# Reciprocals of dt taken row by row instead of in two halves, in a Mamba-2 and mixture-of-experts block

## The chip, the cores and the metric

The kernel runs on one core of a Trainium2 chip, as one launch. The metric is the device time of one execution in microseconds (us). The engines are named as in the profile: PE is TensorE (PEld its weight loads), DVE is VectorE, ACT is ScalarE, POOL is GpSimd, and SP is the queue that issues most DMAs. All data of the computation are 32-bit floats, apart from some counters and masks.

## What is computed

Four rows of 512 tokens with 256 channels pass through an adaLN block: a modulated layer norm, a Mamba-2 mixer, a gated residual, and then a second modulated layer norm with a top-2 mixture of 8 experts and its residual. The part that the change touches is the mixer's `x / dt`:

```python
dt = softplus(A_log)                       # (4, 512, 64): one value per token and head
x_in = x / dt[..., None]                   # x: (4, 512, 64 heads, 8)
y_ssm = ssd_chunk_scan(x_in * dt[..., None], -dt, Bm, Cm, CHUNK)
Du = D[None, None, :, None] * x_in
yf = (y_ssm + Du).reshape(b, L, D_INNER)
out = einsum('bld,ed->ble', yf * silu(z + z_bias), out_proj_w)
```

The scan itself needs only `x`; `1/dt` is wanted for the term `D * x / dt` that is added to the scan's result. `D` has 64 values, one for each head.

## The kernel before, in words

**Tiles.** The 2048 tokens are 16 tiles of 128, four to a row, tile `n = 4*b + i` for row `b` and place `i`. Tokens lie on the partitions, so `dt`, `fu`, `fv` and `fq` are tensors of 128 x 16 tiles x 64 heads (L324 for `fq`). `fq` holds `D / dt`.

**Order of the work.** All five engines run through one list of steps, made by `program_order` (L96 to L148), and each engine takes from a step what is its own, in that order. Engines wait for each other through counting semaphores alone. The list begins with the first norm, row 0's projections and the factors made of `dt`. Then, for each row, four rounds follow, one for each token tile. A round has the steps `tr` (transposes to token layout and the products C times B), `bt`, `z` (y of the tile before, transposed and gated), `state`, `out` (its output projection and residual), `norm` (its second layer norm) and `y` (the tile's scan result), with gaps between them. The gaps are filled by the next row's projections (`p`), its own z projections, and steps of the experts, as the table `GAPS` says. Row 3 has the experts' matmuls in its gaps.

**Taps.** A projection tile (`proj`, L1703 on PE) goes through ACT (L1143, newest tap with bias), then DVE adds the three older taps of the convolution in three instructions (L1315), and ACT applies silu (L1072). DVE does not do the taps in the step `proj` itself but at the end of the next step of the list, or at the next `proj` (L1307, `pending`).

**The reciprocals.** `1/dt` is the step `d_dt`. DVE takes the reciprocal (L1383) and signals `inverse_ready`; POOL multiplies by `D` (L984) and signals `q_ready`. There are two such steps, each for 8 tiles (2 rows, 512 elements a partition): one in the first list, ahead of row 0's last z projection and tile 0, and one after the step `y` of tile 2 of row 0.

```python
if (slot, i, kind) == (0, 2, "y"):
    steps.append(("d_dt", 1))
```

**What uses them.** In the step `tr` POOL waits for `q_ready`, then writes `xv = xtok * fv` (L1013) for the scan and `xtok = xtok * fq` in place (L1017). The wait is before both:

```python
pool.wait_ge(q_ready, n // 8 + 1)
pool.wait_ge(xtok_ready, n + 1)
```

PE needs `xv` for the state products (L1802) and for the scan's products within a chunk (L1833). DVE scales the scan's result by `fu` (L1432) and adds `xtok` (L1439, the "sum of y" below, `ysum_ready`); PE transposes that in the next round's `z` (L1850), DVE gates it (L1448), PE multiplies with the output weights (L1859), and DVE adds the residual (L1457).

**The second norm of a tile.** In the step `out` DVE takes BN_STATS and BN_AGGR of the new residual (L1264, L1265). In the step `norm` POOL makes `rst` from the variance with two instructions (L947, L948), and DVE normalizes with it to `xn` (L1292), at the head of the same step. In the step `y` POOL makes the scaled rows for the experts from `xn` (L957, L958). At the start of a row, in the step `fold_out`, POOL also multiplies the output weights `wog` by a gate (L1025).

**Names of the other steps and tensors.** `gm` are the masked products of C and B (DVE L1394); `st` is the state at the chunk bounds (DVE L1415, L1419, L1420, which reads `scr` and `dec`); `btok` (ACT L1206) is B in token layout; `xtok` (ACT L1199) is x in token layout.

Of the kernel before, what the change touches and what calls it, by code (L numbers as in the profile page):

```python
# [24 lines left out]
P = 128  # L25
BATCH, SEQ, DM = 4, 512, 256
# [69 lines left out]
def program_order():  # L96
# [13 lines left out]
    for slot in range(BATCH):  # L110
# [5 lines left out]
        for i in range(TPB):  # L116
            prev = (slot, i - 1) if i else (slot - 1, TPB - 1)
            gap = 0
            for kind in ("tr", "", "bt", "z", "", "state", "", "out", "", "norm", "y", ""):
                if not kind:  # L120
                    steps += filling(slot, GAPS[slot][i][gap], nxt, z_own, pair_work)
                    gap += 1
                elif kind in ("z", "out", "norm"):
                    if prev[0] >= 0:
                        steps.append((kind,) + prev)
                else:
                    steps.append((kind, slot, i))
                if (slot, i, kind) == (0, 2, "y"):
                    steps.append(("d_dt", 1))
                if i == 0 and kind == "y":  # L130
                    steps.append(("fold_out", slot))
# [130 lines left out]
def adaln_block(nc, x_d, cT_d, wmod_d, win_d, small_d, wo_d, wg1_d, wg2_d,  # L262
# [16 lines left out]
    with ExitStack() as ctx:  # L279
# [116 lines left out]
        fv_f = fv[:, :, :].rearrange("p i h -> p (i h)")  # L396
        fq_f = fq[:, :, :].rearrange("p i h -> p (i h)")
        ident = cst[:, C_ID:C_ID + P]
# [538 lines left out]
        def _(pool):  # L937
# [32 lines left out]
            for step in STEPS:  # L970
# [8 lines left out]
                elif kind == "d_dt":  # L979
                    h = step[1]  # L980
                    fq_h = fq[:, 8 * h:8 * h + 8, :]
                    pool.wait_ge(ld["small"], 16)
                    pool.wait_ge(inverse_ready, h + 1)
                    pool.tensor_tensor(fq_h, fq_h, dh.rearrange("p (o h) -> p o h", o=1).to_broadcast([P, 8, N_HEAD]),  # L984
                                       ALU.mult).then_inc(q_ready, 1)
# [15 lines left out]
                elif kind == "tr":  # L1001
# [3 lines left out]
                    pool.wait_ge(uv_ready, 4)  # L1005
                    pool.wait_ge(q_ready, n // 8 + 1)
                    pool.wait_ge(xtok_ready, n + 1)
# [245 lines left out]
        def _(dve):  # L1253
# [69 lines left out]
            for step in STEPS:  # L1323
# [56 lines left out]
                elif kind == "d_dt":  # L1380
                    h = step[1]
                    dve.wait_ge(dt_ready, h + 1)
                    dve.reciprocal(fq_f[:, halves(h)], dt_f[:, halves(h)]).then_inc(inverse_ready, 1)  # L1383
                elif kind == "proj" and step[2] < N_CONV:
# [650 lines left out]
```

## Time and profile before

| | us |
|---|---|
| median of 3 runs | 457.52 |
| the three runs | 454.83, 457.52, 464.47 |
| the profiled execution, its own time | 455.36 |
| its span, from first to last instruction | 453.1 |
| mean granted TensorE clock, share of full | 0.936 |

The span is what the trace shows; about 2.3 us of the time lie around it. From the trace's stretches: the first norm and row 0's projections take up to 82 us, the token tiles of row 0 from there to 143, those of row 1 to 213, of row 2 to 286, row 3 with the experts of rows 0 to 2 to 414, and row 3's own experts the rest. Times of trace rows count from the span's start.

### The profile page before, as it was taken

To read this page: it belongs to the slowest core of one execution; us is meant where nothing else is said; L and a number is where in the kernel's file an instruction comes from. 1 tells how busy PE (TensorE), PEld (TensorE's weight loads), DVE (VectorE), ACT (ScalarE), POOL (GpSimd) and SP (SyncE) were. 2 spreads that over 40 slices of the span, in tenths; PEclk is the share of its full clock that TensorE was granted. 3 is DMA by queue.
4 is the path that set the end of the run, shared out by engine and by line. 5 is a ranking of instruction groups with operands and counts; after the bars stand their busy time and mean duration, and the time that the engine had idled before them with its cause. 6 is when DMAs were issued, how large, how long until landed. Compare 5 with 4: busy or idle time off the path is not lost.

```text
span 453.1 us, 8779 instructions
## 1 busy us (share of the span) xinstructions
PE 389.9 (86%) x3224; PEld 250.1 (55%) x3224; DVE 285.2 (63%) x624; ACT 166.7 (37%) x291; POOL 138.8 (31%) x170
## 2 busy tenths in 40 slices
PE   7799698888878999698998969696979886978997
PEld 4378343455635556356655545463867775664365
DVE  4733648898895558998458987733645531152566
ACT  1516757542423253333343323122432534443310
POOL 1300200423134334042771131653245100715230
PEclk9859799999989999999999899977999998888999
DMA  8999911100000102000321000036367579877123
GB/s 255 368 385 387 377 65 23 60 14 2 3 2 2 52 21 61 1 2 3 109 57 61 0 4 1 25 119 199 86 207 255 173 224 352 282 265 243 47 70 116
DMA packets 45820, 56.41 MB, mean 124 GB/s; under 512 B 4228, under 2 KB 37676, under 8 KB 45764
## 3 DMA queue, kind: packets, MB, share of 16 engines
q1 hardware_dynamic: 38276, 44.38, 30.0%
q0 software_dynamic: 2304, 6.29, 4.3%
q10 hardware_dynamic: 5184, 4.98, 3.2%
q8 instruction: 36, 0.59, 0.6%
q14 instruction: 20, 0.16, 0.1%
HBM read 32.82 MB, written 22.82 MB: 123 GB/s over the span
## 4 chain that ended last, share of the span: by engine, by line
PE 53%; DVE 27%; issue 7%; DMA 4%; ACT 4%; SPq 3%; POOL 1%; DVEq 0%; ACTq 0%; POOLq 0%
PE ps L1703 14%; DVE conv L1315 13%; PE ps L1759 4%; PE ps L1859 4%; PE ps L1904 4%; PE ps L1922 3%; PE ps L1768 3%; PE ps L1782 3%; PE ps L1629 2%; PE ps L1833 2%; PE ps L1663 2%; DMA conv<-pair_rows 2%; PE ps L1750 2%; PE ps L1802 2%; DMA conv<-x 1%
## 5 line engine op out<-in xcount | busy, mean ns | idle before, releaser
L1703 PE MATMUL ps<-hT,win 128*128 128x512 f32 x256 | 134.3, 653 | 9.1 <-DVE conv L1315 7.9
L1315 DVE SCALAR_TENSOR_TENSOR conv<-ps,small,conv 128x511 f32<-128x511 f32 x144 | 106.8, 746 | 33.8 <-ACT conv L1143 30.4
L1703 PEld LDWEIGHTS ps<-hT,win 128*128 128x128 f32 x256 | 47.8, 204 | 54.0 <-issue 38.0
L1143 ACT ACTIVATE conv<-ps,small 128x512 f32<-128x512 f32 x48 | 37.2, 775 | 78.7 <-PE ps L1703 78.7
L947 POOL TENSOR_SCALAR rst<-mv 128x1 f32<-128x1 f32 x16 | 3.6, 225 | 126.5 <-DVE mv L1265 126.5
L1072 ACT ACTIVATE conv<-conv 128x512 f32<-128x512 f32 x48 | 29.7, 624 | 33.1 <-DVE conv L1315 33.0
L1058 POOL DMA_INDIRECT conv<-pair_out,ysloti x24 | 24.1, 1006 | 42.3 <-DVE x L1586 28.3
L1859 PE MATMUL ps<-wog,yT 128*128 128x256 f32 x128 | 31.2, 387 | 1.6 <-issue 1.6
L1859 PEld LDWEIGHTS ps<-wog,yT 128*128 128x128 f32 x128 | 24.2, 195 | 10.8 <-issue 8.2
L1629 PE MATMUL ps<-cst,conv 128*128 128x128 f32 x128 | 20.6, 285 | 10.4 <-ACT conv L1072 4.5
L1629 PEld LDWEIGHTS ps<-cst,conv 128*128 128x128 f32 x128 | 15.1, 145 | 23.6 <-issue 13.8
L1039 POOL DMA_INDIRECT pair_rows<-hs,sloti x24 | 24.3, 1012 | 6.9 <-issue 6.9
L1759 PE MATMUL ps<-conv,hs 128*128 128x128 f32 x152 | 22.8, 301 | 4.1 <-DMA hs<-w_pair 2.8
L1013 POOL TENSOR_TENSOR xv<-xtok,fv 128x512 f32<-128x512 f32 x16 | 17.5, 1096 | 26.9 <-ACT xtok L1199 26.8
L1759 PEld LDWEIGHTS ps<-conv,hs 128*128 128x128 f32 x152 | 20.4, 210 | 6.3 <-issue 4.8
L1802 PEld LDWEIGHTS ps<-xv,btok 64*64 64x64 f32 x448 | 12.9, 140 | 18.6 <-issue 11.2
L1148 ACT ACTIVATE sz<-ps,small 128x512 f32<-128x512 f32 x16 | 10.9, 684 | 32.3 <-PE ps L1703 20.3
L1802 PE MATMUL ps<-xv,btok 64*64 64x64 f32 x448 | 15.1, 231 | 8.0 <-ACT btok L1206 3.3
L1768 PE MATMUL ps<-hs,conv 128*128 128x256 f32 x76 | 19.8, 397 | 0.9 <-DVE hT L1572 0.8
L1833 PE MATMUL ps<-xv,gm 64*64 64x64 f32 x512 | 18.4, 221 | 2.2 <-PE ps L1820 1.0
L1173 ACT ACTIVATE conv<-ps,bupt 128x128 f32<-128x128 f32 x38 | 11.9, 363 | 20.8 <-PE ps L1759 20.8
L1833 PEld LDWEIGHTS ps<-xv,gm 64*64 64x64 f32 x512 | 16.2, 134 | 4.4 <-PE ps L1820 4.4
(189 smaller groups left out, 615.4 us busy)
## 6 DMA issues: line engine op xcount, KB each, us to landing
pair_rows<-zrow SPq DMA_DIRECT2D x1, 12288.0 KB, 43.3
hs<-w_pair SPq DMA_DIRECT2D x38, 256.0 KB, 4.3
conv<-pair_rows SPq DMA_DIRECT2D x38, 128.0 KB, 2.6
pair_out<-conv ACTq DMA_DIRECT2D x18, 256.0 KB, 4.7
conv<-x SPq DMA_DIRECT2D x4, 512.0 KB, 7.7
wog<-w_out_T SPq DMA_DIRECT2D x4, 512.0 KB
win<-w_in_T SPq DMA_DIRECT2D x2, 512.0 KB, 7.8
hs<-w_mod SPq DMA_DIRECT2D x1, 1024.0 KB, 9.6
```

The costliest lines, as they stand in the source:

```text
L1039: pool.indirect_dma_start(xs_d, bass.IndirectOffsetOnAxis(routed(sloti, b, k, i), 0), hb[b][:, i, :], None, bounds_check=N_SLOT - 1, oob_i ...
L1058: pool.indirect_dma_start(yg[:, n % 4, k, :], None, ys_d[g], bass.IndirectOffsetOnAxis(routed(ysloti, b, k, i), 0), bounds_check=GROUP_TIL ...
L1072: act.activation(dst, dst, ACT.Silu).then_inc(silu_done, 1)
L1143: act.activation(conv[:, b % 2, m, :], bank(step), ACT.Identity, bias=cb[:, m:m + 1], scale=cw[:, m, KSIZE - 1:KSIZE]).then_inc(tap0, 1)
L1315: dve.scalar_tensor_tensor(out=dst, in0=bank(("proj", b, m))[:, 0:SEQ - s], scalar=cw[:, m, KSIZE - 1 - s:KSIZE - s], in1=dst, op0=ALU.mul ...
L1629: ins = pe.transpose(bank(job)[:, tile_cols(j)], conv[:, b % 2, base + j, tile_cols(i)], ident)
L1703: ins = pe.matmul(bank(step), win[:, k, m * P:(m + 1) * P], hT[:, k, b * SEQ:(b + 1) * SEQ], start=(k == 0), stop=(k == KD - 1))
L1759: ins = pe.matmul(bank(step)[:, tile_cols(t % 2)], wt[:, t % W_RING, k * P:(k + 1) * P], hg[:, q % 2, k, tile_cols(t % QUAD)], start=(k == ...
L1768: ins = pe.matmul(bank(step)[:, j * DM:(j + 1) * DM], hq[:, q % 2, tile_cols(t % QUAD)], wt[:, t % W_RING, KD * D_EXP:], start=True, stop= ...
L1802: ins = pe.matmul(ps[64 * par:64 * par + 64, bank_of[job], j * CHUNK:(j + 1) * CHUNK], btok[rows, n % 2, g * 64:(g + 1) * 64], xv[rows, n ...
L1833: last = pe.matmul(ps[rows, bank_of[job], j * CHUNK:(j + 1) * CHUNK], gm[rows, n % 2, par, j * CHUNK:(j + 1) * CHUNK], xv[rows, n % 2, g * ...
L1859: ins = pe.matmul(bank(step)[:, 0:DM], yT[:, n % 2, m, :], wog[:, m, :], start=(m == 0), stop=(m == CT_ - 1))
```

## The change

The step `d_dt` is for one row now, with 4 tiles and 256 elements a partition. Row 0's stands where the first half stood. The others stand in tile 2 of the row ahead (rows 1, 2 and 3 in tile 2 of rows 0, 1 and 2), directly before the step `norm`. POOL's wait in `tr` is for its own row's product.

```diff
@@ program_order, in the loop over rows and tiles
                 elif kind in ("z", "out", "norm"):
+                    if kind == "norm" and i == 2 and slot + 1 < BATCH:
+                        steps.append(("d_dt", slot + 1))
                     if prev[0] >= 0:
                         steps.append((kind,) + prev)
                 else:
                     steps.append((kind, slot, i))
-                if (slot, i, kind) == (0, 2, "y"):
-                    steps.append(("d_dt", 1))
@@ POOL
                 elif kind == "d_dt":
-                    h = step[1]
-                    fq_h = fq[:, 8 * h:8 * h + 8, :]
+                    b = step[1]
+                    fq_b = fq[:, b * TPB:(b + 1) * TPB, :]
                     pool.wait_ge(ld["small"], 16)
-                    pool.wait_ge(inverse_ready, h + 1)
-                    pool.tensor_tensor(fq_h, fq_h, dh.rearrange("p (o h) -> p o h", o=1).to_broadcast([P, 8, N_HEAD]),
+                    pool.wait_ge(inverse_ready, b + 1)
+                    pool.tensor_tensor(fq_b, fq_b, dh.rearrange("p (o h) -> p o h", o=1).to_broadcast([P, TPB, N_HEAD]),
                                        ALU.mult).then_inc(q_ready, 1)
@@ POOL, step "tr"
-                    pool.wait_ge(q_ready, n // 8 + 1)
+                    pool.wait_ge(q_ready, b + 1)
@@ DVE
                 elif kind == "d_dt":
-                    h = step[1]
-                    dve.wait_ge(dt_ready, h + 1)
-                    dve.reciprocal(fq_f[:, halves(h)], dt_f[:, halves(h)]).then_inc(inverse_ready, 1)
+                    b = step[1]
+                    dve.wait_ge(dt_ready, b // 2 + 1)
+                    dve.reciprocal(fq[:, b * TPB:(b + 1) * TPB, :], dt[:, b * TPB:(b + 1) * TPB, :]).then_inc(inverse_ready, 1)
```

A line number of the changed kernel is one less than that of the kernel before from the removed line on. Since `d_dt` is a step of its own, the taps that were pending at `norm` in tile 2 of row 0 are now done at the end of `d_dt`. On DVE, from BN_AGGR of tile 2 of row 0 on, there stood (conv is written by the three taps):

```order
L1265 BN_AGGR mv<-bns 128x2 [waits dve_chain]
L1292 TENSOR_SCALAR xn<-x,mv,rst 128x256 [waits xn_used,var_ready,rstd_ready]
L1315 SCALAR_TENSOR_TENSOR conv<-ps,small,conv 128x511 [waits tap0_written]
L1315 SCALAR_TENSOR_TENSOR conv<-ps,small,conv 128x510 [waits taps_added]
L1315 SCALAR_TENSOR_TENSOR conv<-ps,small,conv 128x509 [waits taps_added]
```

and behind the sum of y of that tile, the reciprocal of 512 elements:

```order
L1439 TENSOR_TENSOR ytok<-ytok,xtok 128x512 [waits ytok_ready,xq_ready]
L1383 RECIPROCAL fq<-dt 128x512 [waits dt_ready]
L1394 TENSOR_TENSOR gm<-ps,cst 128x256 [waits bank3_full,bank6_full]
L1394 TENSOR_TENSOR gm<-ps,cst 128x256 [waits bank4_full]
L1315 SCALAR_TENSOR_TENSOR conv<-ps,small,conv 128x511 [waits tap0_written]
```

Now there stands, from BN_AGGR on:

```order
L1264 BN_AGGR mv<-bns 128x2 [waits dve_chain]
L1382 RECIPROCAL fq<-dt 128x256 [waits dt_ready]
L1314 SCALAR_TENSOR_TENSOR conv<-ps,small,conv 128x511 [waits tap0_written]
L1314 SCALAR_TENSOR_TENSOR conv<-ps,small,conv 128x510 [waits taps_added]
L1314 SCALAR_TENSOR_TENSOR conv<-ps,small,conv 128x509 [waits taps_added]
L1291 TENSOR_SCALAR xn<-x,mv,rst 128x256 [waits xn_used,var_ready,rstd_ready]
L1431 TENSOR_TENSOR ytok<-ps,fu 128x4x64 [waits bank5_full]
```

The reciprocal stands ahead of the taps, the taps ahead of `xn`, and none stands between the sum of y and `gm`. In tile 2 of row 1 (and of row 2, where it reads the same but for a name), DVE had

```order
L1315 SCALAR_TENSOR_TENSOR conv<-ps,small,conv 128x511 [waits tap0_written]
L1315 SCALAR_TENSOR_TENSOR conv<-ps,small,conv 128x510 [waits taps_added]
L1315 SCALAR_TENSOR_TENSOR conv<-ps,small,conv 128x509 [waits taps_added]
L1292 TENSOR_SCALAR xn<-x,mv,rst 128x256 [waits hb_ready,xn_used,var_ready,rstd_ready]
L1432 TENSOR_TENSOR ytok<-ps,fu 128x4x64 [waits bank5_full]
```

and now has

```order
L1314 SCALAR_TENSOR_TENSOR conv<-ps,small,conv 128x511 [waits tap0_written]
L1314 SCALAR_TENSOR_TENSOR conv<-ps,small,conv 128x510 [waits taps_added]
L1314 SCALAR_TENSOR_TENSOR conv<-ps,small,conv 128x509 [waits taps_added]
L1382 RECIPROCAL fq<-dt 128x256 [waits dt_ready]
L1291 TENSOR_SCALAR xn<-x,mv,rst 128x256 [waits hb_ready,xn_used,var_ready,rstd_ready]
L1431 TENSOR_TENSOR ytok<-ps,fu 128x4x64 [waits bank5_full]
```

so here the taps already stood ahead of `xn`, and the reciprocal is between them. On POOL, in the same place of row 1, there stood from the tile before's `xtok` on

```order
L1017 TENSOR_TENSOR xtok<-xtok,fq 128x512 [waits xv_ready]
L947 TENSOR_SCALAR rst<-mv 128x1 [waits var_ready]
L948 TENSOR_TENSOR rst<-rst,half 128x1 [waits pool_chain]
L957 TENSOR_TENSOR hs<-xn,hm 128x256 [waits ld_hm,xn_ready]
L958 TENSOR_TENSOR hs<-hs,hm 128x256 [waits pool_chain]
```

and now

```order
L1016 TENSOR_TENSOR xtok<-xtok,fq 128x512 [waits xv_ready]
L983 TENSOR_TENSOR fq<-fq,small 128x256 [waits inverse_ready,ld_small]
L946 TENSOR_SCALAR rst<-mv 128x1 [waits var_ready]
L947 TENSOR_TENSOR rst<-rst,half 128x1 [waits pool_chain]
L956 TENSOR_TENSOR hs<-xn,hm 128x256 [waits ld_hm,xn_ready]
L957 TENSOR_TENSOR hs<-hs,hm 128x256 [waits pool_chain]
```

POOL's product with `D`, which waits for the reciprocal, is now ahead of `rst`, in rows 0, 1 and 2 alike. PE, ACT and SP have the same instructions in the same order as before.

## Rows read from the trace of the kernel before

**Rows 1.** The page, part 1: busy us, share of the span and instructions.
```profile
PE 389.9 (86%) x3224; PEld 250.1 (55%) x3224; DVE 285.2 (63%) x624; ACT 166.7 (37%) x291; POOL 138.8 (31%) x170
```
**Rows 2.** Chain that ended last: start us, us, engine, tile, line.
```profile
126.64 3.36 DVE fq L1383
...
131.35 1.09 POOL xv L1013
```
**Rows 3.** DVE's timeline, row 0: start us, us, line, operation, count, [idle before, releaser].
```profile
82.20 3.34 DVE L1383 RECIPROCAL fq<-dt 128x512 f32<-128x512 f32 x1
...
87.33 2.31 DVE L1315 SCALAR_TENSOR_TENSOR conv<-ps,small,conv 128x511 f32<-128x511 f32 x3 [1.18 <-ACT conv L1143]
...
90.57 1.35 DVE L1420 TENSOR_TENSOR st<-scr,dec 128x256 f32<-128x256 f32 x1
```
**Rows 4.** PE's timeline at the start of tile 3 of row 0.
```profile
127.33 1.88 PE L1703 MATMUL ps<-hT,win 128*128 128x512 f32 x4
132.53 0.68 PE L1802 MATMUL ps<-xv,btok 64*64 64x64 f32 x16 [3.32 <-POOL xv L1013]
133.14 3.54 PE L1703 MATMUL ps<-hT,win 128*128 128x512 f32 x4
```
**Rows 5.** DVE's timeline, tiles 2 and 3 of row 0.
```profile
121.43 0.18 DVE L1265 BATCH_NORM_AGGREGATE mv<-bns 128x2 f32<-128x6 f32 x1
122.62 0.41 DVE L1292 TENSOR_SCALAR xn<-x,mv,rst 128x256 f32<-128x256 f32 x1 [1.01 <-POOL rst L948]
...
129.90 0.69 DVE L1394 TENSOR_TENSOR gm<-ps,cst 128x256 f32<-128x256 f32 x2
...
138.59 0.42 DVE L1457 TENSOR_TENSOR x<-ps,x 128x256 f32<-128x256 f32 x1 [2.16 <-PE ps L1859]
```
**Rows 6.** POOL's timeline, row 0.
```profile
89.28 2.36 POOL L1025 TENSOR_TENSOR wog<-wog,gates 128x1024 f32<-128x1024 f32 x1
...
123.11 0.73 POOL L957 TENSOR_TENSOR hs<-xn,hm 128x256 f32<-128x256 f32 x1 [0.53 <-DVE xn L1292]
...
130.13 1.27 POOL L984 TENSOR_TENSOR fq<-fq,small 128x512 f32<-128x512 f32 x1 [5.47 <-DVE fq L1383]
```
**Rows 7.** Timelines of POOL, DVE and PE, tiles 2 and 3 of row 1.
```profile
195.71 0.57 POOL L948 TENSOR_TENSOR rst<-rst,half 128x1 f32<-128x1 f32 x1
...
200.99 1.07 POOL L1013 TENSOR_TENSOR xv<-xtok,fv 128x512 f32<-128x512 f32 x1
...
198.58 0.41 DVE L1292 TENSOR_SCALAR xn<-x,mv,rst 128x256 f32<-128x256 f32 x1
...
199.75 0.69 DVE L1439 TENSOR_TENSOR ytok<-ytok,xtok 128x512 f32<-128x512 f32 x1
...
208.47 0.42 DVE L1457 TENSOR_TENSOR x<-ps,x 128x256 f32<-128x256 f32 x1 [0.52 <-PE ps L1859]
...
200.01 0.60 PE L1629 MATMUL ps<-cst,conv 128*128 128x128 f32 x4
200.59 0.63 PE L1850 MATMUL ps<-cst,ytok 128*128 128x128 f32 x4
```
**Rows 8.** Timelines of DVE and PE, tile 3 of row 2 and tile 0 of row 3.
```profile
269.66 0.69 DVE L1439 TENSOR_TENSOR ytok<-ytok,xtok 128x512 f32<-128x512 f32 x1
...
268.26 0.63 PE L1629 MATMUL ps<-cst,conv 128*128 128x128 f32 x4 [1.59 <-issue]
...
269.72 3.59 PE L1703 MATMUL ps<-hT,win 128*128 128x512 f32 x4
...
273.68 0.60 PE L1850 MATMUL ps<-cst,ytok 128*128 128x128 f32 x4
...
295.01 1.61 PE L1802 MATMUL ps<-xv,btok 64*64 64x64 f32 x32 [3.32 <-ACT btok L1206]
296.55 3.78 PE L1703 MATMUL ps<-hT,win 128*128 128x512 f32 x4
```
**Rows 9.** One stretch: busy us of PE, PEld, DVE, ACT, POOL; PEclk, DMA share, GB/s.
```profile
133.00:137.00 4.00, 4.00 (x13) 1.84 (x10) 3.32 (x6) 0.76 (x2) 0.58 (x1) 0.57 0.02 6
```

More of the change, by code:

```diff
@@ L396, in adaln_block @@
         fv_f = fv[:, :, :].rearrange("p i h -> p (i h)")
-        fq_f = fq[:, :, :].rearrange("p i h -> p (i h)")
         ident = cst[:, C_ID:C_ID + P]
```

## The prediction

> **What bounds the kernel now.** I read the page first, then the chain of waits, then the timelines of single engines around the two reciprocals and around the places to which the diff moves them. TensorE (PE) is busy for 86% of the span and VectorE (DVE) for 63% [rows 1]; neither share says what a change in one stage is worth. In the loop over token tiles the chain passes back and forth between the two: DVE's three older taps of a projection tile, PE's projections, and again the taps. So an operation counts only where its engine is the late one. The second reciprocal is such a place. It stands in the chain for 3.36 us, and behind it POOL's products for the next tile, `xv` with 1.09 us the last of them [rows 2]; then PE goes on. The first reciprocal is in no such place, as the next part shows.
>
> **Part 1, the first reciprocal (before tile 0 of row 0).** It runs from 82.20 for 3.34 us. DVE then has two short `gm` products and idles 1.18 us until ScalarE has written a conv tile, at 87.33 [rows 3]. Half as many elements make the reciprocal 1.67 us instead of 3.34 (in proportion; a fixed part could make it a little more). DVE saves 1.67 us and waits longer by as much, for the wait was there already. Worth here: 0. But POOL gets its input 1.67 us earlier and its own product is shorter: 1.27 us for 512 elements a partition [rows 6], and about 0.73 us for 256, the length of a product of that size on POOL at 123.11 [rows 6]; bounds 0.64 (half) and 1.27. So POOL is some 2.2 us ahead, and its scaling of `wog`, now from 89.28 to 91.64 [rows 6], ends near 89.4. In that time DVE's product `st<-scr,dec`, from 90.57, takes 1.35 us [rows 3], where a sum of 256 elements takes 0.42 [rows 5]. If `wog` is done before, DVE gets 0.93 us back, on a stretch in which DVE never idles until PE waits for it. I take -0.9, with 0 as the other end.
>
> The Trainium skill, SBUF — State Buffer, section "Who interferes with whom", says that a VectorE instruction with two SBUF inputs and a GpSimd instruction that reads SBUF exclude each other for the whole of the one that started first. The trace agrees so far: the slow product has both inputs in SBUF and ends when `wog` has ended. By that rule the 0.9 is gained as soon as `wog` ends first; without it the sum would be 0.9 higher.
>
> **Part 2, the second reciprocal leaves the end of tile 2 of row 0.** The order now has a reciprocal of half the size between BN_AGGR and the taps. Before, DVE idles 1.01 us ahead of `xn` for POOL's `rst` [rows 5]. After, the reciprocal starts where the idle time started, at 121.61; the taps follow; and `xn` comes behind them. POOL's product and `rst` need 0.14 + 0.73 + 0.9 = 1.8 us after the reciprocal (0.14 is the step from its end to POOL's start at 130.13, 0.9 is the rest of the 1.01), and the taps cover that with their 2.2 us. So `gm` of the next tile starts not at 129.90 but at 129.90 - 3.26 (126.64 to 129.90) - 1.01 + 1.67 = 127.3: DVE gains 2.6 us. PE idles 3.32 us before 132.53 for `xv`, and after this wait its four projection matmuls take 3.54 us, against 1.88 for the same four at 127.33 [rows 4]: the granted clock is 0.57 from 133 to 137 [rows 9], so for most of that time PE ran at 1.2 GHz of its 2.4. After the change the sum of y is 0.6 us later than before, so those projections start near 127.9 and end near 129.8; `xv` is ready at 128.9 (`xn` near 125.4 plus POOL's 3.5 us from there, as at 198.58 [rows 7]). PE goes on at 129.8 instead of 132.53, 2.7 us earlier, and without the slow stretch, 1.7 us more. The next thing that waits, DVE's sum at 138.59 [rows 5], starts 4.4 us earlier. DVE was free at 136.4 (its idle time there is 2.16 us), now 2.6 us earlier, at 133.8, just before PE's 134.2; so PE is late there, by little. I take -4.4; if the clock still fell it would be -2.7.
>
> **Part 3, a reciprocal and a product more in tile 2 of row 1.** Here no idle time of DVE covers it: `rst` is ready at 196.28 and `xn` starts at 198.58, straight behind the taps [rows 7]. The order puts the reciprocal between taps and `xn`, and on POOL the product ahead of `rst`. POOL's queue is in order, so `rst`, which was 2.3 us early, now waits for the reciprocal; behind it stand the row's scaled rows and the next tile's `xv`. The steps: reciprocal 198.58 to 200.25; POOL from 200.4; product to 201.1; `rst` and `xn` 0.95 later, near 202.1. `xn` is 3.5 us late, and so is all that DVE has behind it. The sum of y, from 199.75, was just in time: PE had to wait about 0.15 us for it before its transposes at 200.59 [rows 7]. Now PE idles some 3.6 us, from 200.45 to 204.1. That is as long as the 3.32 us before 132.53 and the 3.32 us before 295.01, and behind both the projections were slow, 3.54 and 3.78 us [rows 4, 8]. So I add the price of such a stretch, 3.54 - 1.88 = 1.7 us (up to 1.9 by the other). PE is not idle between there and 208.4, and DVE waits for PE at 208.47 [rows 7], so nothing takes it back: +3.5 and +1.7. The end from below is the reciprocal alone, +1.7, if POOL's part could be hidden; nothing in the order hides it.
>
> **Part 4, the same in tile 2 of row 2.** There PE has a pause of 1.59 us that no semaphore explains and soon after it slow projections, 3.59 us [rows 8]; it comes to its transposes only at 273.68 while the sum of y was ready at 270.35 [rows 8]. 3.5 us more on DVE make that 273.9, so PE starts near 274.1: +0.4. If in the new run the pause or the slow stretch before it is absent, DVE still sets 274.1, but PE has then idled over 3 us and its slow stretch comes later: +0.4 + 1.7 = +2.1. I take +0.4.
>
> **Part 5, the rest.** Two more reciprocals of half size add nothing to DVE's sum but two fixed parts; POOL has 4 x 0.73 instead of 2 x 1.27, +0.4 us on an engine busy for 31%. Each starts behind a wait, so it is counted above. The finer wait of each tile's `xv` (for its own row's product) is met long before, as a row's product comes one and a half tiles ahead of use. SP and its DMAs are not moved; they shift with what releases them.
>
> **The sum.** -0.9 - 4.4 + 3.5 + 1.7 + 0.4 = +0.3 us. The profiled execution took 455.4 us with a span of 453.1, so its like would take 455.7. It was the second fastest of the four times shown; against the median of the runs, 457.5, the same sum gives 457.8. I give 456.8, between the two.
>
> **The rivals.**
> *The full clock stays in row 1* (0.15). For it: the fall is not at once, since the 16 products right behind the wait at 132.53 took 0.68 us and only what followed was slow [rows 4]. Against it: both pauses of 3.3 us cost clock, and in row 2 even one of 1.59 us [rows 8]. Then the sum is -1.4 us: 455.1 on the scale of 456.8 for the forecast. This is the faster side.
> *The waits of both rows cost in full* (0.2). PE's pause before row 2's tile 3 is not there, PE waits for the sum of y in both rows, and the clock falls behind both. It decides from the point at which PE waits over 3 us in row 2 as well. Price: +1.7, and +0.2 if the slow stretch is as in row 3: the sum is +2.2, the time 458.7. With `wog` giving nothing, +3.1 and 459.6. This is the slower side.
> *Row 0 gives less* (0.15): something else than `xv` is late at 129.8 (the taps' bank release, or ScalarE's `btok`), PE still idles and its clock still falls, so part 2 is -2.7: the sum is +2.0, 458.5. Against it: the chain of before shows POOL alone ahead of PE there [rows 2, 4].
> *The move does nothing, since the reciprocal costs as much at half size* (0.02): then part 2 loses 1.7 and parts 3 and 4 gain as much more: +0.3 + 1.7 x 3 = +5.4, 461.9.
> The forecast keeps 0.48.
>
> **How the numbers follow.** The cases lie within 455 to 462. To them comes what the trace cannot fix: TensorE's pauses of 1.3 to 1.6 us without a cause in the profile, each of which can bring a slow stretch (two such pairs, 3.3 us each, may come or go with a shift of the order), and the runs' own spread, 454.8 to 464.5. So the range is 451.5 to 462.5. 2% is 9.1 us, about what a measurement of this kernel can tell from no change; no case reaches it, and I leave 0.03 for faster and 0.06 for slower, more there because both new waits sit where an engine is late.
>
> **What would show it.** Four reciprocals of about 1.67 us. In row 0: no wait of PE for `xv` before tile 3, projections at 1.9 us behind it, and a `st` product of 0.42 us. In rows 1 and 2: `xn` idle for POOL's `rst` by about 1.8 us behind the reciprocal, PE idle near 3.6 us before the transposes of y in row 1 with slow projections behind, and a DVE wait in row 2 that PE hardly feels. The forecast is wrong if PE's wait in row 1 is under 2 us, if it runs on at full clock after it, or if row 0 gains under 3 us.

## The result and the profile after

| | before | after |
|---|---|---|
| median of 4 runs each, us | 458.86 | 464.11 |
| lowest and highest, us | 454.83, 464.47 | 462.06, 465.14 |
| profiled execution, its time and span, us | 455.36, 453.1 | 464.07, 462.1 |
| mean granted TensorE clock | 0.936 | 0.922 |

The ratio is 1.0207, with a 95% interval of 1.0134 to 1.0279: the change makes the kernel slower, by 1.1% by the medians and 2.1% by the ratio (experiment 5 gives 1.6% and 1.5%). Medians here and below are over all runs, while ratios compare fast runs alone, those within 1.5% of their kernel's fastest, so the two can differ. The forecast, 456.8 us with a range from 451.5 to 462.5 and nearly all of its chance on no difference, was wrong.

**Busy times say nothing of it.** Part 1 of the page after (busy us, share of the span, instructions), against [rows 1]:

```profile
PE 395.1 (85%) x3224; PEld 252.3 (55%) x3224; DVE 285.8 (62%) x626; ACT 166.1 (36%) x291; POOL 139.0 (30%) x172
```

PE is busy for 5.2 us more with the same 3224 matmuls: it ran a larger part of them at the lower clock. The reciprocals and POOL's products have the lengths that parts 1 and 5 gave them. From the groups of instructions (count | busy us, mean ns | idle before):

```profile
L1382 DVE RECIPROCAL fq<-dt 128x256 f32<-128x256 f32 x4 | 6.9, 1737 | 0.0
...
L983 POOL TENSOR_TENSOR fq<-fq,small 128x256 f32<-128x256 f32 x4 | 2.9, 726 | 80.0 <-DVE fq L1382 80.0
```

**Row 0, DVE after**, against [rows 3, 5] (start us, us, line, operation, [idle before, releaser]):

```profile
76.60 1.74 DVE L1382 RECIPROCAL fq<-dt 128x256 f32<-128x256 f32 x1
...
84.96 0.43 DVE L1419 TENSOR_TENSOR st<-scr,dec 128x256 f32<-128x256 f32 x1
...
115.01 1.72 DVE L1382 RECIPROCAL fq<-dt 128x256 f32<-128x256 f32 x1
116.64 2.22 DVE L1314 SCALAR_TENSOR_TENSOR conv<-ps,small,conv 128x511 f32<-128x511 f32 x3
118.78 0.40 DVE L1291 TENSOR_SCALAR xn<-x,mv,rst 128x256 f32<-128x256 f32 x1
...
127.43 0.42 DVE L1456 TENSOR_TENSOR x<-ps,x 128x256 f32<-128x256 f32 x1 [0.28 <-PE ps L1858]
```

POOL's scaling of `wog`, against [rows 6]:

```profile
81.53 2.37 POOL L1024 TENSOR_TENSOR wog<-wog,gates 128x1024 f32<-128x1024 f32 x1
```

`wog` now ends at 83.90, ahead of the product of `st` at 84.96, and that product is back to 0.43 us from 1.35. `xn` waits for nothing, and PE (next, against [rows 4]) no longer waits for `xv`:

```profile
123.07 0.68 PE L1801 MATMUL ps<-xv,btok 64*64 64x64 f32 x16
123.68 1.98 PE L1702 MATMUL ps<-hT,win 128*128 128x512 f32 x4
```

**Row 1, DVE and then PE after**, against [rows 7]:

```profile
187.41 1.74 DVE L1382 RECIPROCAL fq<-dt 128x256 f32<-128x256 f32 x1
190.90 0.41 DVE L1291 TENSOR_SCALAR xn<-x,mv,rst 128x256 f32<-128x256 f32 x1 [1.75 <-POOL rst L947]
```
```profile
192.91 1.08 PE L1849 MATMUL ps<-cst,ytok 128*128 128x128 f32 x4 [3.48 <-DVE ytok L1438]
193.93 2.07 PE L1738 MATMUL ps<-bdg,sT 8*128 8x256 f32 x4
195.93 3.67 PE L1702 MATMUL ps<-hT,win 128*128 128x512 f32 x4
199.53 0.68 PE L1801 MATMUL ps<-xv,btok 64*64 64x64 f32 x16
200.14 1.98 PE L1702 MATMUL ps<-hT,win 128*128 128x512 f32 x4
```

1.74 us of reciprocal and 1.75 us of waiting for POOL make `xn` 3.5 us late, and PE stands for 3.48 us. Behind the pause everything is slow until 199.5. Three stretches of 4 us (busy us of PE, PEld, DVE, ACT, POOL; PEclk, DMA share, GB/s) show it in the granted clock:

```profile
191.00:195.00 4.00, 2.08 (x7) 1.59 (x8) 3.83 (x9) 0.00 (x0) 3.45 (x4) 0.69 0.01 2
195.00:199.00 4.00, 4.00 (x7) 1.45 (x5) 1.85 (x3) 0.00 (x0) 0.54 (x1) 0.50 0.00 0
199.00:203.00 4.00, 4.00 (x26) 2.35 (x26) 2.64 (x5) 2.08 (x3) 0.00 (x0) 0.96 0.01 4
```

0.50 is 1.2 GHz of 2.4. The chain that ended last, in this stretch (start us, us, engine, tile, line), goes through exactly these steps:

```profile
187.41 1.75 DVE fq L1382
...
189.29 0.73 POOL fq L983
...
190.29 0.58 POOL rst L947
...
192.08 0.70 DVE ytok L1438
...
192.91 1.08 PE ps L1849 x4
```

**Row 2, PE after**, against [rows 8]:

```profile
270.50 0.63 PE L1628 MATMUL ps<-cst,conv 128*128 128x128 f32 x4 [1.45 <-issue]
...
271.96 1.98 PE L1702 MATMUL ps<-hT,win 128*128 128x512 f32 x4
...
277.06 0.63 PE L1849 MATMUL ps<-cst,ytok 128*128 128x128 f32 x4 [2.68 <-DVE ytok L1438]
277.62 1.88 PE L1738 MATMUL ps<-bdg,sT 8*128 8x256 f32 x4
279.43 3.78 PE L1702 MATMUL ps<-hT,win 128*128 128x512 f32 x4
...
284.19 3.78 PE L1702 MATMUL ps<-hT,win 128*128 128x512 f32 x4
```

The pause without a cause is there as before, but the projections behind it took 1.98 us, not 3.59. So PE was ready early, waited 2.68 us for the sum of y, and then had two sets of projections at half clock.

**Where the time went, by stretch.** The cuts are starts of DVE instructions: the first sum of y, then residuals (L1457 of before). Each column is the length of the stretch after, less that of before. The first column is the pair of traces above. Both kernels were traced once more (below): the second column sets the first trace of after against the second of before, the third sets the two second traces against each other.

| stretch | after - before, both 1st traces | after 1st - before 2nd | after 2nd - before 2nd |
|---|---|---|---|
| start to first sum of y | -6.5 | -6.7 | -1.0 |
| to residual in tile 3 of row 0 | -4.6 | -2.4 | -1.9 |
| to residual in tile 2 of row 1 | 0.0 | 0.0 | 0.0 |
| to residual in tile 3 of row 1 | +6.6 | +6.6 | +5.8 |
| to residual in tile 2 of row 2 | +7.0 | +0.6 | -2.0 |
| to residual in tile 3 of row 2 | +5.9 | +9.1 | +7.4 |
| to the last residual of row 3 | +5.2 | -0.1 | +1.2 |
| the rest | -4.6 | -0.3 | -0.1 |
| sum | +9.0 | +6.9 | +9.5 |

The change touches the first, second, fourth and sixth line. The +7.0 and +5.2 of the first column are absent from the others: there the first trace of before was the unusual one, as the section on the hardware shows. The pair that is left, the second trace of after against the first of before, gives +5.8 in the fourth line and +4.3 in the sixth.

### The profile page after: what moved, and what is told of

It is laid out like the page before. It is cut to its first block, busy times and chain, and to the rows that moved or that the text cites. A ratio compares the mean times of both kernels' runs of the same rounds, so it can differ in the third digit from the quotient of the medians.

```text
span 462.1 us, 8785 instructions
## 1 busy us (share of the span) xinstructions
PE 395.1 (85%) x3224; PEld 252.3 (55%) x3224; DVE 285.8 (62%) x626; ACT 166.1 (36%) x291; POOL 139.0 (30%) x172
## 4 chain that ended last, share of the span: by engine, by line
PE 55%; DVE 24%; issue 7%; ACT 5%; DMA 3%; another core or an unknown queue 2%; POOL 2%; SPq 1%; DVEq 0%; ACTq 0%; POOLq 0%
PE ps L1702 16%; DVE conv L1314 11%; PE ps L1858 4%; PE ps L1903 3%; PE ps L1767 3%; PE ps L1921 3%; PE ps L1758 3%; PE ps L1781 3%; PE ps L1832 2%; PE ps L1628 2%; PE ps L1801 2%; PE ps L1869 2%; PE ps L1749 2%; PE ps L1662 2%
## 5 line engine op out<-in xcount | busy, mean ns | idle before, releaser
L1702 PE MATMUL ps<-hT,win 128*128 128x512 f32 x256 | 138.1, 669 | 6.6 <-DVE conv L1314 5.6
L1702 PEld LDWEIGHTS ps<-hT,win 128*128 128x128 f32 x256 | 48.9, 208 | 52.6 <-issue 38.4
L1858 PE MATMUL ps<-wog,yT 128*128 128x256 f32 x128 | 33.5, 408 | 0.7 <-issue 0.7
L1858 PEld LDWEIGHTS ps<-wog,yT 128*128 128x128 f32 x128 | 25.7, 206 | 10.8 <-issue 7.6
L983 POOL TENSOR_TENSOR fq<-fq,small 128x256 f32<-128x256 f32 x4 | 2.9, 726 | 80.0 <-DVE fq L1382 80.0
L1418 DVE TENSOR_TENSOR scr<-ps,st 128x256 f32<-128x256 f32 x24 | 10.1, 422 | 23.8 <-remote 14.2
L1767 PE MATMUL ps<-hs,conv 128*128 128x256 f32 x76 | 21.1, 417 | 1.1 <-DVE hT L1571 0.8
```

What stands on the lines that cost most here:

```text
L1702: ins = pe.matmul(bank(step), win[:, k, m * P:(m + 1) * P], hT[:, k, b * SEQ:(b + 1) * SEQ], start=(k == 0), stop=(k == KD - 1))
L1767: ins = pe.matmul(bank(step)[:, j * DM:(j + 1) * DM], hq[:, q % 2, tile_cols(t % QUAD)], wt[:, t % W_RING, KD * D_EXP:], start=True, stop= ...
L1858: ins = pe.matmul(bank(step)[:, 0:DM], yT[:, n % 2, m, :], wog[:, m, :], start=(m == 0), stop=(m == CT_ - 1))
```

## The experiments

A "piece" is the time from the residual in tile 2 over the sum of y to the residual in tile 3 of a row, on DVE. Ratios are to the kernel before, run on the same chip in the same job.

**1. The kernel before, once more** (no edit).

> The kernel before, unchanged, for a second trace of it. Theory A (the changed kernel is slower because of what its order does in rows 1 and 2): ratio 1.00, and the trace shows the same waits as the first one, with the first token tile starting within 1 us of 82 us. Theory B (the two traces differ by something that comes and goes, such as the start of the first token tile, 5.6 us earlier in the changed kernel's trace, and the late signals of TensorE near 217 to 224 and 350 to 355 us): the trace of this run differs from the first one by several us at such places although nothing was changed, and the spread over the runs is that of before, 9 us.

Measured: median 457.45 us, ratio 1.0029 [0.9959, 1.0100]; nine of the ten runs lie between 454.66 and 464.14 us, the tenth took 553.55. Its trace holds two surprises. Row 0, PE, against [rows 4]:

```profile
132.11 0.68 PE L1802 MATMUL ps<-xv,btok 64*64 64x64 f32 x16 [3.31 <-POOL xv L1013]
132.72 1.98 PE L1703 MATMUL ps<-hT,win 128*128 128x512 f32 x4
```

The same wait of 3.3 us, and no slow clock behind it: 1.98 us instead of 3.54. And row 2, against [rows 8]:

```profile
270.79 0.66 PE L1629 MATMUL ps<-cst,conv 128*128 128x128 f32 x4
...
272.28 1.98 PE L1703 MATMUL ps<-hT,win 128*128 128x512 f32 x4
...
274.68 0.63 PE L1850 MATMUL ps<-cst,ytok 128*128 128x128 f32 x4
...
276.29 1.98 PE L1703 MATMUL ps<-hT,win 128*128 128x512 f32 x4
```

No pause ahead of L1629, no slow projections: the piece takes 14.25 us instead of 17.41. What part 4 counted as cover comes in one execution and not in the next of the same kernel. Over all 14 traces of this document the pause ahead of this place (1.45 to 1.89 us) is there in seven, and slow projections behind it in four of these.

**2. POOL's product last.** The changed kernel with POOL's product as a step of its own behind `norm`, so that `rst` doesn't wait for the reciprocal.

```diff
                     if prev[0] >= 0:
                         steps.append((kind,) + prev)
+                    if kind == "norm" and i == 2 and slot + 1 < BATCH:
+                        steps.append(("d_q", slot + 1))
@@ POOL
-                elif kind == "d_dt":
+                elif kind == "d_q" or step == ("d_dt", 0):
```

> The changed kernel with POOL's product by D put behind rst in tile 2 of every row; DVE's reciprocals stay where they are. Theory A: xn waits no longer for POOL, so rows 1 and 2 lose 1.7 us of their 3.5 us each, and PE's wait in row 1 falls from 3.5 to about 1.8 us, which may leave the clock high: 3.5 to 7 us faster than the changed kernel, ratio to before 1.005 to 1.013. Rival (the slow stretches and late signals are not tied to these waits): the ratio stays at 1.02.

Measured: 462.52 us, 1.0109 [1.0035, 1.0183], 1.6 us under the 464.11 of the changed kernel where 3.5 to 7 were expected. PE's wait in row 1 is 1.61 us instead of 3.48 and nothing behind it is slow; pieces 16.86 us in row 1 and 17.55 in row 2, against 20.84 and 23.35. In row 2 this trace has the pause and the slow projections ahead of the transposes, as the first trace of before had:

```profile
268.83 3.42 PE L1704 MATMUL ps<-hT,win 128*128 128x512 f32 x4
...
272.53 0.60 PE L1851 MATMUL ps<-cst,ytok 128*128 128x128 f32 x4
```

The sum of y comes 1.6 us later than before (7.10 us behind the residual, not 5.53), PE does not wait for it, and the piece is no longer than the 17.41 and 17.46 us of traces with the same slow projections and no delay. So the cover works where it is there; what fails is to count on it. Once more:

> pool_last once more: the changed kernel with POOL's product behind the norm's rst, DVE's reciprocal where the change has it. Theory: only DVE's own 1.7 us delay the sum of y, PE waits 1.6 us instead of 3.5, and behind a wait that short the clock stays full: row 1's piece 16.5 to 17 us, row 2's 15.5 to 17.6; time 2 to 4 us over the kernel with the idle place and 4 to 7 under the changed one: 458 to 461. Rival: the first median (462.5) was right and its 2 us under the changed kernel is all that POOL's order is worth; then 462 to 464.

Measured: 461.10 us, 1.0072 [0.9991, 1.0154], nearer to the range expected (458 to 461) than to the rival's (462 to 464); pieces 17.94 and 16.84. This time a wait of 1.97 us in row 1 had slow projections behind it, while the 1.61 us in row 2 had none:

```profile
192.36 0.63 PE L1851 MATMUL ps<-cst,ytok 128*128 128x128 f32 x4 [1.97 <-DVE ytok L1440]
192.92 1.13 PE L1740 MATMUL ps<-bdg,sT 8*128 8x256 f32 x4
193.98 3.68 PE L1704 MATMUL ps<-hT,win 128*128 128x512 f32 x4
```

So half of the delay is POOL's order. Of the three shorter waits here one had a slow clock behind it. The changed kernel and experiments 5 and 6 have six longer ones (2.68 to 4.17 us) in rows 1 and 2, and all six had it. That points to a price that grows with the wait, on few cases. The medians fall by 2 to 5 us against the two of the changed kernel, which come from other sets of runs; the pieces fall by 2 to 4 us in row 1 and by 4 to 7 in row 2, and both runs lie between the changed kernel and the best one.

**3. Half the change in row 0: the move without the split.** The kernel before, with its second reciprocal (512 elements) ahead of `norm` in tile 2 of row 0.

```diff
                 elif kind in ("z", "out", "norm"):
+                    if (slot, i, kind) == (0, 2, "norm"):
+                        steps.append(("d_dt", 1))
                     if prev[0] >= 0:
@@
-                if (slot, i, kind) == (0, 2, "y"):
-                    steps.append(("d_dt", 1))
```

> The kernel before with one thing of the change alone: the second reciprocal of 512 elements stands ahead of norm in tile 2 of row 0 and not behind y; no reciprocal in rows 1 and 2. Theory A: row 0 gains about 2.5 us less its longer reciprocal, since PE finds xv ready and keeps its clock: 2 to 4 us faster than before, ratio 0.992 to 0.996. Rival (row 0 gains nothing that lasts to the end): ratio 1.00 or above.

Measured: 459.82 us, 0.9985 [0.9869, 1.0101]. The 2 to 4 us expected are not in the time, whose ratio rests on three of the ten runs. Row 0's piece takes 16.86 us, against 18.07 and 16.36 in the two traces of before and 13.43 in the changed kernel: at full size the reciprocal isn't hidden there, and PE waits 2.27 us for the sum of y. At this place it is the size that pays; experiment 8 tries the full size at another.

**4. An idle place for rows 2 and 3.** The changed kernel; row 1's reciprocal stays where the change has it, the other two go behind `tr` of tile 1, where DVE waits for a conv tile of ScalarE.

```diff
-                    if kind == "norm" and i == 2 and slot + 1 < BATCH:
+                    if kind == "norm" and i == 2 and slot == 0:
                         steps.append(("d_dt", slot + 1))
@@
                     steps.append((kind, slot, i))
+                    if kind == "tr" and i == 1 and 0 < slot < BATCH - 1:
+                        steps.append(("d_dt", slot + 1))
```

> The changed kernel with the reciprocals for rows 2 and 3 in tile 1 of the row ahead, behind the products of C and B, where DVE idles 3 us for ScalarE; row 0 is as in the changed kernel. Theory A: rows 1 and 2 cost nothing more, row 0 keeps its gain of 5.5 us: ratio to before 0.985 to 0.992, and PE has no wait for the sum of y in tile 3 of rows 1 and 2. Theory B (late signals of TensorE, or where instructions lie, make the loss): they appear here as well and the ratio is 1.00 to 1.02.

Measured: 454.64 us, 0.9905 [0.9772, 1.0039]; pieces 14.26 and 17.46. Once more:

> The kernel of idle_place once more, for a second trace and a closer ratio. Theory: it has what the change gains in row 0 (about 4 us) and pays nothing in rows 1 and 2 (pieces of 14 to 17.5 us): 3 to 6 us faster than before, ratio 0.987 to 0.995, and 8 to 10 us faster than the changed kernel. Rival: the first ratio of 0.9905 was luck, and it is within 1 us of before.

Measured: 455.67 us, 1.0013 [0.9944, 1.0082]; pieces 15.07 and 16.01. DVE in row 1:

```profile
154.70 1.74 DVE L1384 RECIPROCAL fq<-dt 128x256 f32<-128x256 f32 x1
157.80 2.32 DVE L1316 SCALAR_TENSOR_TENSOR conv<-ps,small,conv 128x511 f32<-128x511 f32 x3 [1.35 <-ACT conv L1144]
```

Even with the reciprocal there, DVE idles 1.35 us more before the taps. The medians are 5.4 and 3.7 us under those of before in the same jobs (460.08 and 459.37), but neither interval excludes no difference, and the second ratio shows none; so a gain over the kernel before is not shown. Against the changed kernel the medians are 9.5 and 10.8 us lower (464.11, from another set of runs, and 466.49, from the same). PE has no wait for the sum of y in rows 1 and 2. The late signals of theory B are in both traces (5.53 and 6.84 us in row 3, see the section on the hardware), so they are not what makes the changed kernel slower.

**5. The changed kernel, once more** (no edit).

> The changed kernel, unchanged. Theory: its loss is real and sits in rows 1 and 2. DVE reaches the normalization (L1291) of tile 2 late by about 3.5 us in both rows, the output transposes of PE (L1849) wait for the sum of y by 2.5 to 3.5 us, and slow projections follow. Both pieces from the sum of y to the output transposes' residual of tile 3 (L1456 to L1456) take 19 to 23 us against 14.3 in a kernel without the wait; row 0's piece takes 7.5 against 10.9 to 12.6. Sum near +6 to +9 us against before in the stages compared: time 464 to 468, ratio to before 1.01 to 1.02. Rival: the 5 us between the two medians came from the few runs of each; then this kernel is within 2 us of before when both have many runs, ratio under 1.005.

Measured: 466.49 us, 1.0148 [1.0034, 1.0261], with 25 runs of before at 459.37. Pieces 20.04 and 21.66 us, PE waits of 3.13 and 4.17 us. The loss stands.

**6. One row's wait at a time.** The kernel of experiment 4, with row 2's reciprocal (issued in row 1) back in the change's place, and in another kernel row 3's (issued in row 2).

```diff
-                    if kind == "norm" and i == 2 and slot == 0:
+                    if kind == "norm" and i == 2 and slot in (0, 1):
@@
-                    if kind == "tr" and i == 1 and 0 < slot < BATCH - 1:
+                    if kind == "tr" and i == 1 and slot == 2:
```

The second has `(0, 2)` and `slot == 1` in these two places.

> The changed kernel with row 3's reciprocal (issued in row 2) at the idle place of DVE in tile 1, and row 2's (issued in row 1) where the change puts it, ahead of the norm of tile 2. Theory: row 1 loses by itself: its piece from L1456 to L1456 around the sum of y of tile 2 takes 19 to 21 us against 14.3, while row 2's stays at 14 to 17.5 us. Time 5 to 7 us over idle_place, so 459 to 462. Rival of the record (its part 3): +5.2 here. Rival that only the last wait before row 3 costs: within 2 us of idle_place.

> The reverse: row 3's reciprocal (issued in row 2) ahead of the norm of tile 2 as in the change, row 2's (issued in row 1) at the idle place of tile 1. Theory: row 2 pays the wait in full and about as much as row 1: its piece takes 20 to 23 us against 14 to 17.5, with PE waiting 2.5 us or more for the sum of y and two slow stretches of projections; time 5 to 7 us over idle_place. Rival (the record's part 4, PE is held up there anyway): +0.4, at most +2.1; the time is within 2 us of idle_place and the piece takes at most 18 us.

Measured: row 1 alone 460.01 us, 1.0042 [0.9982, 1.0102], row 1's piece 20.69 and row 2's 15.00 us; row 2 alone 460.68 us, 1.0037 [0.9955, 1.0119], row 1's piece 14.26 and row 2's 24.17 us. Against the idle place's 455.67 in the same job that is +4.3 and +5.0 (5 to 7 were expected for each); together +9.3, and the changed kernel with both is at +10.8. Over the runs that the ratios use the medians give +3.3, +1.1 and +11.0, so the times leave row 2's own price open between 1.1 and 5.0 us. The trace of row 2 alone is also of the slowest of its ten runs (466.32 us; they go from 453.08). But the two traces of the changed kernel have nearly the same piece in row 2 (23.35 and 21.66 us): in the traces each row pays by itself, and row 2 no less than row 1. PE with row 2 alone:

```profile
274.72 1.08 PE L1851 MATMUL ps<-cst,ytok 128*128 128x128 f32 x4 [4.16 <-DVE ytok L1440]
...
277.73 3.78 PE L1704 MATMUL ps<-hT,win 128*128 128x512 f32 x4
...
282.49 3.78 PE L1704 MATMUL ps<-hT,win 128*128 128x512 f32 x4
```

**7. POOL's part alone.** The kernel of experiment 4, with the products of rows 2 and 3 ahead of `norm` of tile 2 and the reciprocals still at the idle place.

```diff
                     if kind == "norm" and i == 2 and slot == 0:
                         steps.append(("d_dt", slot + 1))
+                    if kind == "norm" and i == 2 and slot in (1, 2):
+                        steps.append(("d_q", slot + 1))
@@ POOL
-                elif kind == "d_dt":
+                elif kind == "d_q" or kind == "d_dt" and step[1] < 2:
```

> The kernel of idle_place with POOL's products of rows 2 and 3 directly ahead of the norm of tile 2, where the change has them, while DVE's reciprocals stay at the idle place. POOL then has 0.73 us more ahead of rst, but waits for nothing. Theory: in row 1 rst was 2.3 us early, so nothing moves; at most 0.7 us in either row; the time is within 1 us of idle_place (454 to 457). What costs in the change is not POOL's work but that rst stands behind a product that waits for DVE. Rival: POOL's queue is the late one by itself; then both rows lose 0.7 us and PE's wait grows with a slow stretch behind: 457 to 460.

Measured: 457.71 us, median of only 4 runs (450.61 to 468.97), so the time decides nothing; the trace does. Both pieces take 14.26 us, as in the second trace of before (14.26 and 14.25), and no other trace has less. POOL's 0.73 us is no cost by itself. What cost 1.75 us was that `rst` stood behind an instruction that waits for DVE.

**8. The second half in the idle place.** The kernel before, with nothing else edited:

```diff
-                if (slot, i, kind) == (0, 2, "y"):
+                if (slot, i, kind) == (1, 1, "tr"):
                     steps.append(("d_dt", 1))
```

> The kernel before, with nothing but the place of its second reciprocal changed: still 512 elements for rows 2 and 3, now in tile 1 of row 1 behind the step tr, where DVE idles 2.7 us for a conv tile (3.36 us against 2.7, so up to 0.7 us are felt). Theory: the whole gain is that row 0's end is free of the reciprocal: piece of row 0 from the sum of y of tile 2 to the residual 7.5 to 9 us against 10.9 to 12.6, rows 1 and 2 as before; time 1 us over idle_place (wog still beside the product of st) and 2 to 4 under before. Rival: the splitting into rows is what pays, and this kernel stays within 1 us of before.

Measured: median of its ten runs 459.27 us, beside 460.45 for before: 0.3% less. The ratio comes out as 0.9819 [0.9746, 0.9892], but it rests on three of the ten runs, which spread from 448 to 470 us, so I read nothing from it. Row 0's piece is 13.66 us, as good as with the change, and without any split; but in this trace the next tile took 1.7 us more, behind projections of 3.51 us that followed a pause of 1.47 us. The expected 2 to 4 us are not confirmed.

**9. Filling PE's wait.** The changed kernel, with six matmuls more on PE ahead of its wait for the sum of y in tile 2 of rows 1 and 2. They write to the bank that the transposes overwrite.

```diff
                     wait_bank_free(pe, step)
+                    if i == 2 and b in (1, 2):
+                        for _ in range(6):
+                            pe.matmul(bank(step)[:, 0:SEQ], win[:, 0, 0:P], hT[:, 0, b * SEQ:(b + 1) * SEQ],
+                                      start=True, stop=True)
                     pe.wait_ge(ysum_ready, n + 1)
```

> The changed kernel, with six matmuls of 128x512 more on PE in rows 1 and 2, ahead of its wait for the sum of y of tile 2, into the bank that the transposes behind the wait overwrite; the result is the same. They fill some 2.8 us of the 3.5 us in which PE stood idle. Theory: DVE's delay stays (3.5 us in each row: L1418 to L1438 pieces as in the changed kernel, L1438 near 9.0 us after L1456), but the slow stretches behind it go, since they come from PE's pause: granted clock near 1.0 behind the wait, four projections 1.9 us instead of 3.7, and the piece from L1456 over L1438 to L1456 takes 17.5 to 18.5 us in row 1 instead of 20 to 21, in row 2 18 to 20 instead of 22 to 24. Time 4 to 6 us under the changed kernel: 459 to 461. Rival: the slow stretches come from something else (the total of PE's work, or the place), then the fill changes nothing or, with six matmuls at half clock, costs 1 to 3 us a row: 465 to 470.

Measured: 470.54 us, 1.0267 [1.0156, 1.0378]. The experiment was badly sized, on two counts that its PE rows show:

```profile
197.48 7.11 PE L1849 MATMUL ps<-hT,win 128*128 128x512 f32 x12 [2.26 <-DVE ytok L1431]
204.43 0.60 PE L1853 MATMUL ps<-cst,ytok 128*128 128x128 f32 x4
204.96 1.13 PE L1738 MATMUL ps<-bdg,sT 8*128 8x256 f32 x4
206.01 1.98 PE L1702 MATMUL ps<-hT,win 128*128 128x512 f32 x4
...
282.64 5.42 PE L1849 MATMUL ps<-hT,win 128*128 128x512 f32 x12 [2.40 <-DVE ytok L1431]
```

Six matmuls of 32-bit floats are 12 records and 5.42 us, twice what I had counted. And their bank comes free only with DVE's scaling (L1431), 2.3 us into the pause: most of the wait could not be filled. Behind the fill the clock is full in both rows, but in row 1 the fill itself ran slow for a while (7.11 us). In row 2 PE stood for 2.40 us and no slow stretch came at all; in row 1 it stood for 2.26 us and one came. So this doesn't separate the pause from the slow clock, and no version that fills the pause from its start was tried.

## Why the prediction was wrong

**Part 1** held: -0.9 expected; the first reciprocal to the first sum of y takes 11.78 us after and 12.72 before, because `wog` ends first and the `st` product takes 0.43 us.

**Part 2** held in its mechanism: each step named came as described. The size depends on the trace taken as before. Against the first it is -4.6 us (-4.4 expected). The second trace of before has the same wait of 3.31 us without the slow stretch, and its piece is 16.36 us, not 18.07. Their mean less 13.43 gives -3.8.

**Part 3** held in its mechanism, and its second term was too small. DVE's delay was 3.50 us (9.03 from residual to sum of y, 5.53 before), as worked out. But the slow stretch is not one set of projections. It cost 3.08 us (11.81 - 8.73): transposes 1.08 instead of 0.63, the expert bias products 2.07 instead of 1.13, projections 3.67 instead of 1.98, which is 0.45 + 0.94 + 1.69. I had priced 1.7. In the second trace of after it was the projections alone, and 1.65 us (10.38 - 8.73); row 1 alone had 2.93. Mean over the traces: 20.52 us with the wait (three kernels' traces) and 14.46 without (eight), +6.1 where +5.2 was expected.

**Part 4 is the step that failed.** It read: PE comes to its transposes only at 273.68, so 3.5 us more on DVE give +0.4. Measured: +5.9, +9.1, +7.4 and +4.3 in the four pairs of traces; on the mean, 23.06 us with the wait (three traces) and 15.95 without (eight), so +7.1; +5.0 by the medians of experiment 6, where the runs that the ratio uses give only +1.1. The cover was a slow set of projections of one execution. The eight traces without the wait have pieces from 14.25 to 17.46 us, so the clock fell in some and not in others. I had even written "if the pause or the slow stretch is absent", and priced that case at +2.1. That was wrong by its own logic: without the slow stretch before is itself some 3 us faster, so the case costs the whole 3.5 us plus a slow stretch, as in row 1. None of the three traces with the wait had the cover; experiment 2's first trace had it, and there a delay of 1.6 us cost nothing.

**The rival** "waits of both rows cost in full" names what happened. It had 0.2, and its time, 458.7, carried the same mistaken base. With the measured sizes its sum is -0.9 - 3.8 + 6.1 + 7.1 = +8.5 us. That lies inside both measured intervals (1.0134 to 1.0279 and 1.0034 to 1.0261 of some 459 us, so 6 to 13 and 2 to 12 us). The medians themselves give +5.3 and +7.1. The rival of a full clock behind row 1's wait did not come: in all three traces of it the clock fell. Rival "row 0 gains less" is half right, by the second trace of before.

**The base** was 2 us low: 456.8 lay between one execution and the median of three runs, while the medians of before in the later jobs are 460.08, 459.37 and 460.45. The forecast was 456.5 + 0.3. So the miss of 7.3 us is 2.4 of base (458.86 - 456.5) and 4.9 of change (5.2 measured by the medians less the 0.3 of the sum).

**The signs named beforehand** for row 1 (PE idle near 3.6 us, slow projections) and for row 0 were all there; the one for row 2, a wait that PE hardly feels, was not, and there the profile says at once which step failed.

## What to carry to other kernels

An engine's lateness in one trace is cover for added work only if the cause of the lateness is in the program: a semaphore wait or a queue. If it is a stretch at lower clock or a pause that no semaphore explains, take a second trace before counting on it, and price the edit on the version without it. Where an in-order engine (here POOL) gets an instruction that waits for another engine, everything behind inherits the wait: put it behind the short operations on which others depend, and put the operation that it waits for where its engine idles for an input anyway.

## What the runs showed of the hardware that was not expected

**The clock behind a pause is likely, not certain.** Between 80 and 310 us the 14 traces have 21 pauses of PE of 3.1 to 4.2 us. Behind 18 of them a set of four projections took 2.9 to 3.8 us instead of 1.9; behind three (3.31, 3.32 and 3.25 us long) it did not. Pauses of 1.4 to 2 us show both, in one and the same kernel. The count makes it likely that the pause causes the fall; it was not tested apart, since the fill failed.

**The start has two speeds.** From 20 to 40 us, which no edit here touches, the granted clock (the column behind POOL's, 0.97 and 0.74) differs; the changed kernel first, then the second run of before:

```profile
20.00:40.00 20.00, 18.47 (x118) 14.30 (x116) 9.88 (x19) 11.34 (x17) 1.25 (x2) 0.97 1.08 385
```
```profile
20.00:40.00 20.00, 18.18 (x84) 13.75 (x83) 8.05 (x17) 6.15 (x11) 1.25 (x2) 0.74 1.08 385
```

Four traces of the 14 have 0.97 to 1.00 there and their first sum of y at 88.4 to 89.7 us, the other ten 0.74 and 93.1 to 95.8. The changed kernel is in both groups (88.38 and 94.05), so the -6.5 us of the table's first line are not its merit, apart from 0.9.

**Late signals.** In tile 0 of row 2 and in row 3, DVE waits for something that the profile names only "remote". From the changed kernel:

```profile
217.58 0.42 DVE L1418 TENSOR_TENSOR scr<-ps,st 128x256 f32<-128x256 f32 x1 [2.10 <-remote]
...
352.02 0.42 DVE L1418 TENSOR_TENSOR scr<-ps,st 128x256 f32<-128x256 f32 x1 [5.41 <-remote]
```

The second run of before has the same in row 2:

```profile
220.09 0.42 DVE L1419 TENSOR_TENSOR scr<-ps,st 128x256 f32<-128x256 f32 x1 [1.89 <-remote]
```

Such waits are in 13 of the 14 traces; the first trace of before, from which the forecast was read, has none. In row 3 the stretch from the sum of y of tile 1 to the residual behind it takes 18.6 to 20.8 us in the 13 and 14.99 in that one. What is late was not tried; it is no effect of the change.
